# Score stacks that pair two areas of one head in place of two heads of one area

## What is computed

```
g = clip((n * ac_w + ac_b) * n, 0, 6)            # n: group norm of x
q, k, v = einsum('bchw,dc->bdhw', g, qkv_w)      # 3 x 16 heads x 8, cut into windows of 64 tokens
attn = softmax(einsum('wnqd,wnkd->wnqk', q, k) * hd ** -0.5)
o = einsum('wnqk,wnkd->wnqd', attn, v)
x = x + einsum('bchw,dc->bdhw', o, proj_w) + proj_b
x = x + conv3x3(groupnorm(x)) + bias             # second layer
```

## Time and profile before

| | |
|---|---|
| median of 3 runs | 1206.1 us (1197.05 to 1206.22) |
| the profiled execution | 1207.08 us, its span 1205.3 us |
| TensorE matmuls busy | 1015.8 us, 84% of the span |
| DVE / ACT / GpSimd busy | 82% / 66% / 42% |
| granted TensorE clock, mean | 0.947 |
| attention of image 1 / image 2 | about 50 to 456 us / 656 to 1046 us |

### The profile page before, as it was taken

One profiled execution on the slowest core, in us unless ns is written; L12 is line 12 of the kernel. 1 busy time (PEld: TensorE's weight loads), 2 busy tenths in 40 slices (PEclk: granted clock), 3 DMA queues, 4 the chain that ended last, 5 costly groups with the idle time before them and its releaser, 6 DMA issues.

```text
span 1205.3 us, 52690 instructions
## 1 busy us (share of the span) xinstructions
PE 1015.8 (84%) x23011; PEld 582.6 (48%) x23011; DVE 983.1 (82%) x1312; ACT 791.3 (66%) x1327; POOL 503.8 (42%) x469
## 2 busy tenths in 40 slices
PE   0388999999999985998853899999999999779996
PEld 0155565556555652433321555556655655334442
DVE  6786888889888754899986788888988976379996
ACT  1257787778778774655532688878887877556663
POOL 5214454445444433233343245545454544404335
PEclk9879999999999997999986899999999999879998
DMA  8234444444444420133343454444444444001112
GB/s 307 84 118 125 136 138 138 136 137 128 135 142 135 142 64 1 44 129 108 105 157 122 123 150 139 136 137 138 144 132 148 134 142 126 4 1 53 70 70 88
DMA packets 114917, 140.59 MB, mean 117 GB/s; under 512 B 25088, under 2 KB 91008, under 8 KB 113664
## 3 DMA queue, kind: packets, MB, share of 16 engines
q1 hardware_dynamic: 114688, 137.23, 36.3%
HBM read 67.96 MB, written 67.11 MB: 112 GB/s over the span
## 4 chain that ended last, share of the span: by engine, by line
PE 63%; DVE 18%; issue 8%; DMA 4%; ACT 3%; SPq 2%; POOL 2%; POOLq 0%; DVEq 0%; ACTq 0%
PE ps L918 11%; PE ps L899 11%; PE ps L926 9%; PE ps L885 8%; PE ps L995 6%; PE ps L853 5%; DVE work L760 5%; PE ps L854 5%; PE ps L855 5%; DVE work L756 4%; PE ps L872 4%; DVE st L610 1%; SPq L288 1%; DVE work L738 1%; DMA q_bd<-stack_scratch 1%
## 5 line engine op out<-in xcount | busy, mean ns | idle before, releaser
L654 DVE TENSOR_REDUCE m_all<-ps 128x16 f32<-128x1024 f32 x256 | 313.5, 1225 | 114.9 <-PE ps L885 114.3
L370 POOL TENSOR_SCALAR work<-work 128x256 f32<-128x256 f32 x128 | 108.6, 849 | 401.2 <-DVE work L647 352.4
L885 PEld LDWEIGHTS ps<-k_pl,q_bd 48*64 48x64 f16 x8192 | 90.4, 111 | 174.5 <-issue 126.9
L448 ACT ACTIVATE late_probs<-ps,ws 128x1024 f32<-128x1024 f32 x128 | 142.8, 1116 | 44.6 <-PE ps L899 42.8
L853 PE MATMUL ps<-work,c_hi 128*128 128x512 f16 x384 | 148.3, 386 | 27.7 <-DVE work L760 27.7
L899 PE MATMUL ps<-q_bd,k_pl 128*64 128x256 f16 x2048 | 163.8, 282 | 7.5 <-ACT work L448 4.0
L885 PE MATMUL ps<-k_pl,q_bd 48*64 48x64 f16 x8192 | 118.6, 198 | 57.3 <-issue 39.4
L536 ACT CAST work<-work 128x512 f16<-128x512 f32 (+1 forms) x128 | 79.0, 622 | 115.8 <-DVE work L756 107.9
L448 ACT ACTIVATE work<-ps,ws 128x1024 f32<-128x1024 f32 x128 | 141.7, 1107 | 13.1 <-PE ps L899 11.5
L854 PE MATMUL ps<-work,c_lo 128*128 128x512 f16 x384 | 148.0, 385 | 0.0
L855 PE MATMUL ps<-work,c_hi 128*128 128x512 f16 x384 | 147.4, 384 | 0.0
(11 more groups left out here) (126 smaller groups left out, 1894.1 us busy)
## 6 DMA issues: line engine op xcount, KB each, us to landing
stack_scratch<-work SPq DMA_DIRECT2D x128, 256.0 KB, 2.4
q_bd<-stack_scratch SPq DMA_DIRECT2D x256, 96.0 KB
k_pl<-stack_scratch SPq DMA_DIRECT2D x128, 192.0 KB, 3.5
stack_scratch<-work SPq DMA_DIRECT2D x128, 128.0 KB, 2.5
out_dram<-work SPq DMA_DIRECT2D x32, 512.0 KB, 2.9
img<-in_x_dram SPq DMA_DIRECT2D x8, 1024.0 KB, 13.4
img<-in_x_dram SPq DMA_DIRECT2D x16, 512.0 KB, 4.3
q_bd<-m_pair SPq DMA_DIRECT2D x256, 8.0 KB
```

The source lines that it names most:

```text
L370: g.tensor_scalar(near[h], near[h], -2.0, None, ALU.add).then_inc(less_done, 1)
L448: a.activation(probs[h][:, p % 2, :], ps[:, ST_B:ST_B + 2, :].rearrange("p w t -> p (w t)"), ACT.Exp, scale=ws[:, R_EXP:R_EXP + 1]).then_i ...
L654: v.tensor_reduce(m_all[:, 0, :, p], ps[:, S_B:S_B + 2, :].rearrange("p r (a k) -> p (r a) k", k=WIN), AX.X, ALU.max).then_inc(max_done, 1)
L885: mm = t_.matmul(ps[64 * w:64 * w + 64, S_B + r, at:at + WIN], q_bd[rows, md, r, g, j, tok], k_pl[rows, md, g, tok], start=True, stop=True)
```

## The change

A stack now holds one head of two neighbouring windows (`HE` = 2): 8 channels x 2 windows x 3 parts = 48 rows. Each half of the rows holds eight such stacks (`HG` = 8). The query stack has the 128 queries of both windows along the free axis, with zeros in the rows of the other window; the key stack has the 64 keys of one window in the rows of the first and of the other in those of the second. One plain score matmul has 128 stationary columns (the queries of both windows) and 64 moving ones (the keys), so `scores` has 16 matmuls per pair of windows in place of 32, on two tiles of 64 rows x 128 columns. The zeros of q are no longer kept in `q_bd`: they are set once per image in the SBUF source (`q_flat`, one memset by GpSimd, for which ACT's first q copy of the image waits), and written to DRAM and read back with the rest. `scores_t` keeps its 8 matmuls of 128 x 64 x 256 and their order; v, the weights of the projection and the probabilities change only in the order of their columns, so that one DMA loads `proj_w` in place of two.

```diff
-HR, HG, HJ = 2, 4, 2
+HR, HG, HJ, HE = 2, 8, 2, 2
-ROWS = HJ * HD * PARTS
-HROWS = HD * PARTS
+ROWS = HE * HD * PARTS
...
-    stackd = nc.dram_tensor("stack_scratch", [BUFS, 2, P, PARTS, UT], F16, kind="Internal").ap()
+    q_stack = nc.dram_tensor("q_stack", [BUFS, P, HE, PARTS, UT], F16, kind="Internal").ap()
+    k_stack = nc.dram_tensor("k_stack", [BUFS, P, HE, PARTS, UT // HE], F16, kind="Internal").ap()
...
-        k_pl = sb("k_pl", [P, BUFS, HG, UT], F16)
+        k_pl = sb("k_pl", [P, BUFS, HG, UT // HE], F16)
-        q_bd = sb("q_bd", [P, BUFS, HR, HG, HJ, UT], F16)
+        q_bd = sb("q_bd", [P, BUFS, HR, HG, UT], F16)
...
+        q_parts = q_flat[:, 0:2 * HE * UT].rearrange("p (e s t) -> p e s t", e=HE, s=2)
+        def queries(s):
+            both = q_flat[:, s * UT:s * UT + HE * (2 * UT + WIN)].rearrange("p (e y) -> p e y", e=HE)[:, :, 0:UT]
+            return both.rearrange("p e (a f t) -> p a e f t", a=PAIRS, f=HE)[:, :, :, 0, :]
+        def keys(s):
+            return k_parts[:, :, s, :].rearrange("p e (a t) -> p a e t", a=PAIRS)
...
-                    sp.dma_start(to[:, 0:2, :], qk[:, 2 * which:2 * which + 2, :]).then_inc(sent, 16)
-                    sp.dma_start(to[:, 2, :], qk[:, 1 + which, :]).then_inc(sent, 16)
+                    sp.dma_start(q_stack[md, :, :, 0:2, :].rearrange("p e s t -> p e (s t)"),
+                                 q_parts.rearrange("p e s t -> p e (s t)")).then_inc(q_sent, 16)
+                    sp.dma_start(q_stack[md, :, :, 2, :], q_parts[:, :, 1, :]).then_inc(q_sent, 16)
...
+                    sp.dma_start(k_stack[md, :, :, 0:2, :].rearrange("p e s x -> p e (s x)"),
+                                 k_parts.rearrange("p e s x -> p e (s x)")).then_inc(k_sent, 16)
+                    sp.dma_start(k_stack[md, :, :, 2, :], k_parts[:, :, 0, :]).then_inc(k_sent, 16)
...
                     for r in range(HR):
-                        for j in range(HJ):
-                            at = 64 * r + HROWS * j
-                            sp.dma_start(q_bd[at:at + HROWS, md, r, :, j, :], q_rows[r, j]).then_inc(q_in, 16)
+                        sp.dma_start(q_bd[64 * r:64 * r + ROWS, md, r, :, :], q_rows[r]).then_inc(q_in, 16)
...
-                    k_rows = stackd[md, 1].rearrange("(r g a) s t -> r (a s) g t", r=HR, g=HG)
+                    k_rows = k_stack[md].rearrange("(r g d) e s x -> r (d e s) g x", r=HR, g=HG)
...
             for b in range(BATCH):
+                if b:
+                    after(pool, out_done, b * CUNITS - 3)
+                    g.memset(q_flat[:, 0:2 * HE * UT].bitcast(F32), 0.0).then_inc(q_zero, 1)
...
                     for g in range(HG):
-                        for j in range(HJ):
-                            for w in range(EACH):
-                                tok = slice((EACH * p + w) * WIN, (EACH * p + w + 1) * WIN)
-                                at = g * P + j * WIN
-                                for r in range(HR):
-                                    rows = slice(64 * r, 64 * r + ROWS)
-                                    mm = t_.matmul(ps[64 * w:64 * w + 64, S_B + r, at:at + WIN],
-                                                   q_bd[rows, md, r, g, j, tok], k_pl[rows, md, g, tok],
-                                                   start=True, stop=True)
+                        for r in range(HR):
+                            rows = slice(64 * r, 64 * r + ROWS)
+                            mm = t_.matmul(ps[:, S_B + r, g * WIN:g * WIN + WIN],
+                                           q_bd[rows, md, r, g, p * P:p * P + P], k_pl[rows, md, g, p * WIN:p * WIN + WIN],
+                                           start=True, stop=True)
...
```

More of the change, by code:

```diff
@@ L244, in _ @@
             sp.dma_start(raw_qkv, qkv_w.rearrange("(t d) c -> d t c", t=3)).then_inc(w_in, 16)
-            for c in range(2):
-                sp.dma_start(raw_proj.rearrange("o (a j c d) -> o a j c d", j=HJ, c=2, d=HD)[:, :, :, c, :],
-                             proj_w.rearrange("o (a c j d) -> o a c j d", c=2, j=HJ, d=HD)[:, :, c, :, :]).then_inc(w_in, 16)
+            sp.dma_start(raw_proj, proj_w).then_inc(w_in, 16)
             sp.dma_start(raw_conv, conv_w.rearrange("o i h w -> o i (h w)")).then_inc(w_in, 16)
@@ L299, in one @@
                         after(sp, q_in, n + 1)
-                        write(0, n + 4, (m + 4) % BUFS, q_lo_done, q_sent)
+                        write_queries(n + 4, (m + 4) % BUFS)
                         after(sp, k_in, n + 1)
-                        write(1, n + 4, (m + 4) % BUFS, k_lo_done, k_sent)
+                        write_keys(n + 4, (m + 4) % BUFS)
                 iterations(b, one)
@@ L494, in one @@
                         after(act, k_sent, n + 2)
-                        a.copy(qk[:, 2, :], ps[:, GB, :]).then_inc(k_hi_done, 1)
+                        a.copy(keys(0), by_window(GB)).then_inc(k_hi_done, 1)
                     if live(1):
@@ L865, in v_rows @@
                 def v_rows(md):
-                    r_hi, r_lo = (r[:, 2, :].rearrange("p (k c x) -> p c k x", c=2, x=HJ * HD) for r in (w_hi, w_lo))
+                    r_hi, r_lo = (r[:, 2, :] for r in (w_hi, w_lo))
                     for a in range(PAIRS):
@@ L894, in scores_t @@
                         pe.wait_ge(weights_done, MATS // 4)
[L895 to L901, removed]
+                    for g in range(HG):
+                        k, c = g // 2, g % 2
+                        mm = t_.matmul(ps[64 * c:64 * c + 64, ST_B + k // 2, (k % 2) * 256:(k % 2) * 256 + 256],
+                                       k_pl[:, md, g, p * WIN:p * WIN + WIN], q_bd[:, md, :, g, p * P:p * P + P],
+                                       start=True, stop=True)
                     mm.then_inc(st_done, 1)
@@ L911, in weigh, with pair @@
                         after(pe, quot_out, d - 1, h + 1)
-                    strips = [(2 * r + a, P * r + 256 * a) for r in range(HR) for a in range(2)]
+                    def pair(k, j):
+                        return 512 * (k % 2) + 256 * j + P * (k // 2)
                     for w in range(EACH):
@@ L915, in weigh @@
                         for j in range(HJ):
-                            for k, col in strips:
-                                col += 512 * w + WIN * j
+                            for k in range(HP // HJ):
+                                col = pair(k, j) + w * WIN
                                 mm = t_.matmul(ps[32 * k:32 * k + 32, PV_B + h, at:at + WIN],
@@ L923, in weigh @@
                         for j in range(HJ):
-                            for k, col in strips:
-                                col += WIN * j
-                                mm = t_.matmul(ps[32 * k:32 * k + 32, PV_B + h, HALF:2 * HALF], adds[:, j, :], sums_of(h, col),
+                            for k in range(HP // HJ):
+                                mm = t_.matmul(ps[32 * k:32 * k + 32, PV_B + h, HALF:2 * HALF], adds[:, j, :],
+                                               probs[h][:, :, pair(k, j):pair(k, j) + P],
                                                start=(j == 0), stop=(j == HJ - 1))
                     mm.then_inc(pv_done, 1)
-                def sums_of(h, col):
-                    return probs[h].rearrange("p s (w x) -> p (s w) x", w=EACH)[:, :, col:col + WIN]
                 def one(i, m, live):
```

34 lines of the change are left out of this document (20 added, 14 removed).

## The result

The changed kernel takes **1367.1 us** (median of 4 runs, 1360.95 to 1374.13), the kernel before 1204.4 beside it: a ratio of 1.137 [1.129, 1.144]. The forecast was 1274 with a range to 1330. The direction was right, the size was not: +163 us in place of +68.

The account below looks back on a forecast made before the run. Attention was taken as bound by q and k's trip through DRAM, 13.0 to 15.3 us against 13.3 that TensorE leaves. -4 + 70 + 3 - 1 = +68 on 1207.1 gave 1275, median 1274 us, range 1208 to 1330.

Parts of the forecast that it names:

- (a): Plain scores on TensorE: four phases give -0.14 us per unit, half of it seen, -4 us; ends -9 and +50.
- the rival with slow weights: Plain score matmuls: the 48 x 128 weight load takes the slow way, +25 us on the forecast, about 1300; chance 0.15.
- (b): Writes of q to DRAM: bytes double, +1.1 us until they are sent; k's shorter pieces 0 to +0.4.
- (c): Reads of q: two DMAs for four save 0.8 us of issue; the doubled bytes take 2.8 to 4.1 us.
- the first rival: Reads of q: hidden after all, saved issue and better engine filling pay for the writes; 1207 within 12, chance 0.15.
- (d): Reads of k: same bytes in 512 B pieces for 1 KB, 1.4 to 2.0 us; before 1.5 to 2.
- The trip: q and k through DRAM, per unit of attention: longer by 1.0 to 3.0 us in the mean, 2.0 taken.
- (e): Attention's period: 2.0 us of trip times 0.6 seen, 1.2 per unit, 58 periods: +70 us; ends +29 and +139.
- (f): Start-up: the first two trips of each image have no cover, 2 x 0.8 x 2 = +3 us.
- (g): Added waits of ACT's q and k copies: zero, k up to 0.3 us per unit; one weight DMA less: -1 us.
- the sign that the prediction named for its failing: ACT idle ahead of its q or k copy, ended by a DRAM write, would say the added wait took over.
- The *faster* rival: q reads' issue in the trip: two issues make long ones rare, -22 us, scores -5; about 1180, chance 0.08.

Follow-up runs that it names:

- the run with 24 rows: The changed kernel with each q read cut into two DMAs of 24 rows, same bytes: 1366.9 us, ratio 1.141.
- the kernel with both halvings and narrow matmuls: The changed kernel with half of q's reads and half of q's writes, each paired score matmul cut into its two windows: 1206.2 us, ratio 1.004.
- The kernel with both halvings: The changed kernel with q reads fetching four of eight stacks and, after three units, one of q's two halves written in turn: 1186.25 us, ratio 0.984.

## Why the prediction was wrong in size

*What bounds the kernel* was right: attention's period is set by the trip of q and k, which stood at the edge. Giving the kernel before the new traffic of q gives +195; halving q's bytes in the changed kernel takes all of the loss away.

*(a) Scores.* The floor is 316.53 - 305.53 = 11.00 us against 11.13, as forecast (-0.14), the phase 303.73 - 303.39 = 0.34 as forecast, the 48 x 128 load 101 ns, as short as the 100 ns of the full load; the rival with slow weights is out. (The Trainium skill's section that the prediction names there, "Weight-path perf modes" of "TensorE: Matmul & The Clock Gate", has the 128 columns and the type; that column tiling turns the fast load off does not stand in that section, and nothing here rests on it.) But the worth of it was mis-sized: -20 at the old traffic and -38 at the new, against -4, with -9 as the far end. The halving ("half is seen while the trip binds") was wrong, and I had given fewer instructions no worth beyond the phase. With this the kernel is 1367 in place of 1405.

*(b) Writes of q.* Taken +1.1 us; alone they cost 3.84 - 2.39 = +1.45. The mechanism was right, the size a quarter short. k's writes cost about +0.5 alone (2.9 for two writes of k against 2.4 for those of q before, of as many bytes), and nothing that the runs of the whole kernel show.

*(c) Reads of q.* **This is the term that failed.** The issue fell as said (0.82 for both). For the data I had 2.8 to 4.1 us; its low end brought 186 GB/s "at a share of 0.65" up to a share of 1, as if idle engines meant spare rate. They did not: 192 at 0.63 and 181 at 1.02 are nearly the same rate, and at 181 the data takes 4.3 us, above even the high end. Then I let the mean grow by less, on account of rarer long issues. Alone the read costs 6.5 - 3.77 = **+2.7 us**, the issue's saving included. The Trainium skill's rule on the number of engines ("DMA: Bandwidth & Descriptors", section "Why a DMA increments its semaphore by 16 and not by 1"), named at the first rival, explains the share and not the rate; the run with 24 rows is unchanged.

*(d) Reads of k:* 3.79 against 3.93 alone. Right, at nothing.

*The trip* so grows by 1.45 + 2.7 = 4.2 us, not by 1.0 to 3.0 with 2.0 taken. SyncE's timelines of the two whole kernels say nearly the same. On average over 60 units, q's first read is issued 2.95 us behind the second write before and 4.50 after (the 2.1 that the prediction read is the shortest, not the usual one), and k's reads 2.39 and 1.53 us behind q's; k lands 3.5 and 6.8 us after its issue. Together that is +1.55 - 0.86 + 3.3 = 4.0 us.

*(e) Seen in the period.* 181 us by 62 is 2.9 per unit, by 4.2 a ratio of 0.70; I had 0.6 in a range of 0.5 to 0.8. Right. Of the 181, the sum had 70; 2.2 more of trip at 0.6 are another 77; the rest is the ratio and the four units that I left out.

*(f) Start.* +3 was taken; outside the periods the profiled executions differ by the 8 us above, waits and drain included. No run parts them.

*(g) Added waits and the weight DMA* (0, -1): the kernel with both halvings and narrow matmuls, which has all of them, stands at 1206.2. Right within what these runs can tell. Yet the sign that the prediction named for its failing, idle time of ACT ended by a write to DRAM, is there in the waits of after, ahead of k's copy (L518), in 8 of 64 units; before, it was 1.2 us:

```profile
ACT work L518 <- DMA k_stack<-work: 7.1, 8, 2.3
```

7.1 us in all can't be what makes the 163, and the two halvings, which leave k as it is, take the loss away.

So +163 is -20 for the pairing at the old traffic and +181 for q's bytes, within 2 us. The *faster* rival had a true mechanism, that the pairing is worth something, and the wrong source for it. What was to show the forecast right came out beyond it: the period 14.6 for 13.2, idle time 176 for over 100, k's landing 6.8 for over 4.5, q's first read 4.0 behind the second write for 3.2, the queue's share 56.9% for 49%. The bytes were right: 187.55 - 137.23 = 50.3 MB.

Not settled: how much of the pairing's gain is instruction loading and how much the shorter phase. Not tried: a version that pairs and keeps the zeros on chip, which would have the traffic of before. The kernel with both halvings, at 1186, which leaves half of the scores out, shows about what it could bring.

## What to carry to other kernels

A DMA rate seen at a low share is not that rate divided by the share: look for what else may be at its limit, and measure the transfer by itself before a change hangs on it. Where a round trip is at the edge of its cover, a microsecond on it costs some 0.7 per period. Zeros that travel along as padding are paid for at that price; here the larger matmuls that they make possible won back only a tenth to a fifth of it (20 of 181 us, 38 of 199). A wait for a landing belongs in a queue with nothing behind it that is needed.

## What was unexpected of the hardware

- Reads into 48 rows of one half move 181 GB/s at a share of 1.02 with nothing beside them; into 128 rows 291 (there in pieces of 6 KB), by two queues into both halves 275. Writes out of 128 rows move 361.
- A read in DMAs of 24 rows takes 6.4 us, in DMAs of 48 rows 6.5.
- 4096 matmuls fewer, of 64 moving columns each (4096 of 128 weight columns in place of 8192 of 64), were worth 20 us at the old traffic and 38 us at the doubled one.
